# Handing the sums of x and the residual add of an LSTM to GpSimd, step by step

## The chip, the cores and the metric

The kernel runs on one core of one Trainium2 chip. The metric is the device time of one execution in microseconds (us). A core has a matrix engine (TensorE, PE in the profile, its weight loads shown apart as PEld), VectorE (DVE), ScalarE (ACT), GpSimd (POOL) and SyncE (SP), which here issues the transfers of x and of the output. The engines run their own instruction streams and meet at semaphores.

## The reference

An LSTM layer over 512 steps with a residual: `x` is 32 x 512 x 512 (batch, time, features), the state has 512 features, the weights are 512 x 2048 each.

```python
xW = einsum('ntd,dk->tnk', x, Wx) + b
def step(carry, xw_t):
    prev_h, prev_c = carry
    a = xw_t + prev_h @ Wh
    i, f, o = sigmoid(a[:, :H]), sigmoid(a[:, H:2*H]), sigmoid(a[:, 2*H:3*H])
    g = tanh(a[:, 3*H:])
    next_c = f * prev_c + i * g
    next_h = o * tanh(next_c)
    return (next_h, next_c), next_h
out = x + transpose(hs, (1, 0, 2))
```

Step t+1 cannot begin its product with `Wh` before step t has its `h`. The product with `Wx` does not depend on `h` and can be made ahead.

## The kernel before, in words

**Layout.** Batch (32) and the four blocks of 128 features share the 128 partitions, so a step's `h` is a 128x128 tile. Every float32 operand of a product is split in two float16 parts, "hi" and "lo" (the remainder), and hi·hi, hi·lo and lo·hi are added up in PSUM.

**Two products per step.** `recur` (L240) is the product with `Wh`: 96 matmuls of 256 columns, first for the gates i and f (bank `if_even` or `if_odd`), then for o and g (bank `og_even` or `og_odd`). It waits for `hT_hi`, the transposed float16 part of the last `h`, and before its third block of 16 matmuls for `hT_lo`, the transposed remainder. The product with `Wx` (`product`, L207) is made for two steps (a pair) at a time with seven half-size products instead of eight, Strassen-Winograd fashion. It needs, besides the blocks A11, A12, A21, A22 of x, the sums S1 to S4: S1 = A21 + A22, S3 = A11 - A21, S2 = S1 - A11, S4 = A12 - S2. The seven products are 24 matmuls each, 168 for a pair. They are spread after the `recur` of each of the two steps: `middle` and `close_odd` after an even step, `close_even` and `open_pair` after an odd one.

**What makes x ready.** Steps are counted s = 0 to 7 in a chunk of 8; a group is 4 steps, and `x_ring` holds 4 chunks, loaded by SyncE. For the group two ahead, ScalarE copies 128x512 of x to `x_now` (`copy_x`), VectorE transposes its two halves into `x_blocks` (`transpose_x`, L443) at steps 0 and 1 of a group, forms S1 and S3 at step 1 (`combine_first`) and S2 and S4 at step 2 (`combine_rest`), all by line 454. Later ScalarE casts the blocks to `xT_hi` (`cast_early`, `cast_late`), and VectorE takes the remainders `xT_lo` (`rest_early` L465, `rest_late` L471).

**The step on VectorE** (`step`, L492) in program order: f_c = f·c (L497), i_g = i·g (L499), c_state (L501), a PSUM addition for the Winograd sums (L478 or L489), h_hi = o·tanh(c) in float16 (L509), its transpose hT_hi (L440), h_full, the same product in float32 (L512), h_lo = h_full - h_hi (L515), its transpose hT_lo (L440), another PSUM addition (L484, even steps), the remainders of x (L473 or L468), and then the work for x ahead. At the fourth step of a group one instruction of 128x512 adds the four `h_full` tiles onto the ring (L535) and releases the output transfers.

```python
ring = x_ring[:, ring_of(group)]
nc.vector.tensor_tensor(ring, ring, h_full[:, :, :].rearrange("p r f -> p (r f)"),
                        ALU.add).then_inc(out_ready, GROUP)
```

**What sets the order.** All is written out by hand; each engine runs its instructions in the order of the text, and counting semaphores hold the engines together. SyncE waits for `out_ready` to reach a whole chunk before it stores it. GpSimd has no work. Before the steps there is a part in which VectorE and ScalarE split the weights in hi and lo.

Of the kernel before, what the change touches and what calls it, by code (L numbers as in the profile page):

```python
# [10 lines left out]
P = 128  # L11
# [26 lines left out]
def lstm_residual(nc, x, h0, w_x, w_h, bias, out):  # L38
# [20 lines left out]
    with ExitStack() as ctx:  # L59
# [6 lines left out]
        def sem(name):  # L66
            return ctx.enter_context(nc.semaphore(name))
# [49 lines left out]
        c_zeroed = sem("c_zeroed")  # L117
        x_now_ready = sem("x_now_ready")
        x_blocks_ready = sem("x_blocks_ready")
        early_hi_ready = sem("early_hi_ready")  # L120
        early_ready = sem("early_ready")
        late_hi_ready = sem("late_hi_ready")
# [28 lines left out]
        def steps(engine, step, body=CHUNK, begin=0):  # L151

            with nc.Fori(begin, T // body - 1, engines=(engine,), hint_back_edge=True) as c:
                for s in range(body):
                    step(c * body + s, s, body, c)
            for s in range(body):
                step(T - body + s, s, body - 1 - s, T // body - 1)

        def ring_of(group):

            return bass.ds(group % (RING // GROUP) * (GROUP * P), GROUP * P)
# [162 lines left out]
        def _(act):  # L324
# [10 lines left out]
                nc.scalar.activation(x_now[:, :], x_ring[:, ring_of(group)], ACT.Copy).then_inc(x_now_ready, 1)  # L335

            def cast_early(group, pair):
                act.wait_ge(x_blocks_ready, group * 6 + 6)
                nc.scalar.activation(xT_hi[:, pair % 2, EARLY, :], x_blocks[:, pair // 2 % 2, pair % 2, F_EARLY, :],
                                     ACT.Copy).then_inc(early_hi_ready, 1)  # L340

            def cast_late(group, pair):
                act.wait_ge(x_blocks_ready, group * 6 + 6)
                nc.scalar.activation(xT_hi[:, pair % 2, LATE, :], x_blocks[:, pair // 2 % 2, pair % 2, F_LATE, :],  # L344
                                     ACT.Copy).then_inc(late_hi_ready, 1)

            def step(t, s, left, c):
# [20 lines left out]
                if s % GROUP == 0 and left >= CHUNK:  # L368
                    if s == 0:
                        act.wait_ge(x_loaded, (c + 2) * X_DMA)  # L370
                    act.wait_ge(x_blocks_ready, (c * 2 + s // GROUP) * 6 + 12)
                    copy_x(c * 2 + s // GROUP + 2)
                if s % 2 == 0 and left >= 5:
                    act.wait_ge(a22_done, q + 1)
# [62 lines left out]
        def _(dve):  # L437
            def transpose_h(ready, part, to, done, count):
                dve.wait_ge(ready, count)
                nc.vector.transpose(to[:, :].rearrange("p (k e) -> p k e", k=J),  # L440
                                    part[:, :].rearrange("p (e k) -> p k e", k=J)).then_inc(done, 1)
# [6 lines left out]
                dst = x_blocks[:, g % 2, :, first:first + 5:4, :]  # L448
                nc.vector.transpose(dst, src[:, :, odd, :, :]).then_inc(x_blocks_ready, 1)  # L449

            def combine(group, g, to, a, b, op, after):
                blocks = x_blocks[:, g % 2, :, :, :]
                dve.wait_ge(x_blocks_ready, group * 6 + after)
                nc.vector.tensor_tensor(blocks[:, :, to, :], blocks[:, :, a, :], blocks[:, :, b, :],  # L454
                                        op).then_inc(x_blocks_ready, 1)

            def combine_first(group, g):
                combine(group, g, S1, A21, A22, ALU.add, 2)
                combine(group, g, S3, A11, A21, ALU.subtract, 2)

            def combine_rest(group, g):
                combine(group, g, S2, S1, A11, ALU.subtract, 3)
                combine(group, g, S4, A12, S2, ALU.subtract, 5)

            def rest_early(q, pair):  # L465

                dve.wait_ge(early_hi_ready, q + 1)
# [24 lines left out]
            def step(t, s, left, c):  # L492
# [15 lines left out]
                if left:  # L508
                    nc.vector.tensor_tensor(h_hi[:, :], o_gate[:, :], tanh_c[:, :],  # L509
                                            ALU.mult).then_inc(h_hi_ready, 1)  # L510
                    transpose_h(h_hi_ready, h_hi, hT_hi, hT_hi_ready, t + 2)
                nc.vector.tensor_tensor(h_now, o_gate[:, :], tanh_c[:, :], ALU.mult).then_inc(h_full_ready, 1)  # L512
                dve.wait_ge(h_full_ready, now)
                if left:
# [9 lines left out]
                if left >= CHUNK:  # L524
                    ahead, g = group + 2, s // GROUP
                    if s % GROUP == 0:
                        transpose_x(ahead, g, 0)
                    if s % GROUP == 1:
                        transpose_x(ahead, g, 1)
                        combine_first(ahead, g)  # L530
                    if s % GROUP == 2:
                        combine_rest(ahead, g)
                if s % GROUP == GROUP - 1:
                    ring = x_ring[:, ring_of(group)]
                    nc.vector.tensor_tensor(ring, ring, h_full[:, :, :].rearrange("p r f -> p (r f)"),  # L535
                                            ALU.add).then_inc(out_ready, GROUP)

            def split_lo(src, hi, lo):
                return nc.vector.scalar_tensor_tensor(out=lo, in0=src, scalar=WSCALE, in1=hi,  # L539
# [33 lines left out]
            for group in range(2):  # L573
                transpose_x(group, group, 0)
                transpose_x(group, group, 1)
                combine_first(group, group)
                combine_rest(group, group)
            for pair in range(2):
                rest_early(pair, pair)
                rest_late(pair, pair)  # L580
# [38 lines left out]
                split_h_lo(k)  # L619
            rest_early(2, 2)  # L620
            dve.wait_ge(c_zeroed, 1)
            steps(mybir.EngineType.DVE, step)


# [20 lines left out]
```

## Time and profile before

| what | value |
|---|---|
| median of 3 runs | 2577.95 us (2577.83 to 2578.16) |
| the profiled execution's own time | 2577.3 us |
| its span in the trace | 2575.5 us |
| TensorE busy | 2528.3 us (98%) |
| VectorE busy | 1959.4 us (76%) |
| ScalarE busy | 1023.6 us (40%) |
| GpSimd busy | 0.2 us (0%) |
| mean granted TensorE clock | 0.991 of full speed |

The span runs from the first to the last instruction of one profiled execution. The execution's own time is 1.8 us more, and the median of the unprofiled runs 0.65 us above that. Busy shares are means over the whole span. The slice table of the page shows that all slices look alike after the first, which holds the splitting of the weights (PE at 4 tenths there and at 9 after it).

### The profile page before, as it was taken

How to read it: one execution, taken by the hardware profiler on the slowest of the kernel's cores; microseconds unless marked ns; L12 is line 12 of the kernel's file. 1: busy time of each engine (PE TensorE's matmuls, PEld its weight loads, DVE VectorE, ACT ScalarE, POOL GpSimd, SP SyncE). 2: the span in 40 equal slices, each digit the busy share in tenths (PEclk: the TensorE clock that was granted, in tenths of full speed). 3: DMA queues.
4: the chain of work that ended last, by engine and by line, in shares of the span. 5: the costliest groups of instructions: out<-in, count | busy, mean ns of one | idle time of the engine just before them, and what ended most of it. 6: DMA issues, size and time to landing. Idle time of an engine off the chain costs nothing.

```text
span 2575.5 us, 201412 instructions
## 1 busy us (share of the span) xinstructions
PE 2528.3 (98%) x92166; PEld 2445.7 (95%) x92166; DVE 1959.4 (76%) x6328; ACT 1023.6 (40%) x3231; POOL 0.2 (0%) x4
## 2 busy tenths in 40 slices
PE   4999999999999999999999999999999999999998
PEld 3999999999999999999999999999999999999997
DVE  8777777777777777777777777777777777777775
ACT  5334343333433433343334334333433333343342
POOL 0000000000000000000000000000000000000000
PEclk6999999999999999999999999999999999999999
DMA  4011010010110110100101101101101011011000
GB/s 169 18 33 32 16 33 24 24 33 16 33 33 16 33 33 16 33 24 24 33 19 30 33 16 33 33 16 33 27 22 33 22 27 33 16 33 33 16 16 18
DMA packets 141209, 76.17 MB, mean 30 GB/s; under 512 B 8452, under 2 KB 140164, under 8 KB 140164
## 3 DMA queue, kind: packets, MB, share of 16 engines
q1 hardware_dynamic: 140480, 75.53, 11.0%
q10 hardware_dynamic: 708, 0.33, 0.1%
q8 instruction: 17, 0.28, 0.0%
q14 instruction: 4, 0.03, 0.0%
HBM read 42.27 MB, written 33.55 MB: 29 GB/s over the span
## 4 chain that ended last, share of the span: by engine, by line
PE 98%; DVE 2%; issue 0%; DMA 0%; ACT 0%; ACTq 0%; DVEq 0%
PE if_odd L214 26%; PE if_odd L221 13%; PE og_odd L221 13%; PE og_even L221 13%; PE if_even L221 13%; PE s1t_sum L214 7%; PE if_even L214 6%; PE og_even L214 6%; DVE xw_lo L539 1%; DVE w_raw L564 0%; DVE hw_lo L539 0%; DMA h_raw<-in_cond_dram 0%; DVE x_blocks L449 0%; DVE x_blocks L454 0%; ACTq L394 0%
## 5 line engine op out<-in xcount | busy, mean ns | idle before, releaser
L499 DVE TENSOR_TENSOR i_g<-i_f,g_gate 128x128 f32<-128x128 f32 x512 | 149.7, 292 | 429.4 <-ACT g_gate L354 429.4
L214 PE MATMUL if_odd<-xw_hi,xT_hi 128*32 128x256 f16 x8192 | 403.1, 273 | 29.9 <-DVE xw_lo L539 24.3
L214 PE MATMUL if_odd<-xw_lo,xT_hi 128*32 128x256 f16 x8192 | 403.0, 273 | 0.0
L214 PE MATMUL if_odd<-xw_hi,xT_lo 128*32 128x256 f16 x8192 | 403.0, 273 | 0.0
L214 PEld LDWEIGHTS if_odd<-xw_hi,xT_hi 128*32 128x32 f16 x8192 | 219.8, 97 | 36.5 <-DVE xw_lo L539 31.8
L362 ACT ACTIVATE tanh_c<-c_state 128x128 f32<-128x128 f32 x512 | 158.5, 310 | 193.6 <-DVE c_state L501 193.6
L214 PEld LDWEIGHTS if_odd<-xw_lo,xT_hi 128*32 128x32 f16 x8192 | 220.3, 97 | 5.0
L214 PEld LDWEIGHTS if_odd<-xw_hi,xT_lo 128*32 128x32 f16 x8192 | 220.2, 97 | 5.0
L331 ACT ACTIVATE if_even<-if_odd 128x256 f32<-128x256 f32 x256 | 94.2, 368 | 260.1 <-PE if_odd L214 260.1
L351 ACT ACTIVATE i_f<-if_odd 128x256 f32<-128x256 f32 x256 | 98.7, 386 | 225.5 <-PE if_odd L221 225.5
L344 ACT ACTIVATE xT_hi<-x_blocks 128x256 f16<-128x256 f32 x256 | 106.5, 416 | 192.5 <-PE if_odd L214 192.5
L440 DVE STREAM_TRANSPOSE hT_hi<-h_hi 128x128 f16<-128x128 f16 x512 | 161.1, 315 | 17.4
L440 DVE STREAM_TRANSPOSE hT_lo<-h_lo 128x128 f16<-128x128 f16 x512 | 159.8, 312 | 17.4
L497 DVE TENSOR_TENSOR f_c<-i_f,c_state 128x128 f32<-128x128 f32 x512 | 148.5, 290 | 31.6 <-ACT i_f L351 9.9
L351 ACT ACTIVATE i_f<-if_even 128x256 f32<-128x256 f32 x256 | 98.6, 385 | 180.8 <-PE if_even L221 180.8
L449 DVE STREAM_TRANSPOSE x_blocks<-x_now 128x256 f32<-128x256 f32 x256 | 167.1, 653 | 0.0
L354 ACT ACTIVATE g_gate<-og_odd 128x128 f32<-128x128 f32 x256 | 71.3, 279 | 237.1 <-PE og_odd L221 237.1
L354 ACT ACTIVATE g_gate<-og_even 128x128 f32<-128x128 f32 x256 | 71.2, 278 | 237.1 <-PE og_even L221 237.1
L509 DVE TENSOR_TENSOR h_hi<-o_gate,tanh_c 128x128 f16<-128x128 f32 x511 | 149.1, 292 | 19.2 <-ACT tanh_c L362 0.4
L501 DVE TENSOR_TENSOR c_state<-i_g,f_c 128x128 f32<-128x128 f32 x512 | 149.5, 292 | 17.4
L515 DVE TENSOR_TENSOR h_lo<-h_full,h_hi 128x128 f16<-128x128 f32 x511 | 149.3, 292 | 17.6
L221 PE MATMUL if_even<-hw_lo,hT_hi 128*32 128x256 f16 x4096 | 157.0, 273 | 4.9 <-DVE hw_lo L539 4.8
(78 smaller groups left out, 5812.3 us busy)
## 6 DMA issues: line engine op xcount, KB each, us to landing
x_ring<-in_x_dram SPq DMA_DIRECT2D x256, 128.0 KB, 2.8
out_dram<-x_ring SPq DMA_DIRECT2D x252, 128.0 KB, 2.1
w_raw<-in_L_cond_Wx_dram SPq DMA_DIRECT2D x4, 1024.0 KB, 7.7
w_raw<-in_L_cond_Wh_dram SPq DMA_DIRECT2D x4, 1024.0 KB, 15.5
out_dram<-x_ring SPq DMA_DIRECT2D x8, 64.0 KB, 1.8
bias_raw<-in_L_cond_b_dram ACTq DMA_DIRECT2D x4, 64.0 KB, 4.0
h_raw<-in_cond_dram ACTq DMA_DIRECT2D x1, 64.0 KB
```

What stands on the lines that cost most here:

```text
L214: mm = nc.tensor.matmul(bank[j * N:(j + 1) * N, 0:HALF], x_part[:, pair, n, k * N:(k + 1) * N], w_part[:, n, k, j, :], start=start and g = ...
L221: mm = nc.tensor.matmul(bank[j * N:(j + 1) * N, 0:HALF], hT[:, k * N:(k + 1) * N], w[:, k, j, half * HALF:(half + 1) * HALF], start=False, ...
L351: nc.scalar.activation(i_f[:, :], i_f_bank[:, 0:2 * P], ACT.Sigmoid, scale=UNSCALE).then_inc(if_ready, 1)
L354: nc.scalar.activation(g_gate[:, :], og_bank[:, P:2 * P], ACT.Tanh, scale=UNSCALE).then_inc(g_ready, 1)
L362: nc.scalar.activation(tanh_c[:, :], c_state[:, :], ACT.Tanh).then_inc(tanh_c_ready, 1)
L440: nc.vector.transpose(to[:, :].rearrange("p (k e) -> p k e", k=J), part[:, :].rearrange("p (e k) -> p k e", k=J)).then_inc(done, 1)
L449: nc.vector.transpose(dst, src[:, :, odd, :, :]).then_inc(x_blocks_ready, 1)
L497: nc.vector.tensor_tensor(f_c[:, :], i_f[:, P:2 * P], c_state[:, :], ALU.mult)
L499: nc.vector.tensor_tensor(i_g[:, :], i_f[:, 0:P], g_gate[:, :], ALU.mult).then_inc(i_g_ready, 1)
L501: nc.vector.tensor_tensor(c_state[:, :], i_g[:, :], f_c[:, :], ALU.add).then_inc(c_ready, 1)
L509: nc.vector.tensor_tensor(h_hi[:, :], o_gate[:, :], tanh_c[:, :], ALU.mult).then_inc(h_hi_ready, 1)
L515: nc.vector.tensor_tensor(h_lo[:, :], h_now, h_hi[:, :], ALU.subtract).then_inc(h_lo_ready, 1)
```

## The change

The four sums of x go from VectorE to GpSimd with the same shapes and the same order. Their semaphore is a new one, `x_sums_ready`, for which ScalarE's casts wait; `x_blocks_ready` now counts the transposes alone. The residual addition of 128x512 at every fourth step becomes one of 128x128 at every step, on GpSimd, as soon as that step's `h_full` is there. Since GpSimd reads `h_full` later than VectorE goes on, VectorE waits, before it writes an `h_full` tile again, for the addition of four steps ago. The first chunk of VectorE's steps is written out, so that this wait's value is a positive one.

```diff
             def cast_early(group, pair):
-                act.wait_ge(x_blocks_ready, group * 6 + 6)
+                act.wait_ge(x_sums_ready, group * 4 + 4)
...
-                    act.wait_ge(x_blocks_ready, (c * 2 + s // GROUP) * 6 + 12)
+                    act.wait_ge(x_blocks_ready, (c * 2 + s // GROUP) * 2 + 4)
                     copy_x(c * 2 + s // GROUP + 2)
...
+                if not isinstance(t, int) or t >= GROUP:
+                    dve.wait_ge(out_ready, t - (GROUP - 1))
                 nc.vector.tensor_tensor(h_now, o_gate[:, :], tanh_c[:, :], ALU.mult).then_inc(h_full_ready, 1)
...
                         transpose_x(ahead, g, 1)
-                        combine_first(ahead, g)
-                    if s % GROUP == 2:
-                        combine_rest(ahead, g)
-                if s % GROUP == GROUP - 1:
-                    ring = x_ring[:, ring_of(group)]
-                    nc.vector.tensor_tensor(ring, ring, h_full[:, :, :].rearrange("p r f -> p (r f)"),
-                                            ALU.add).then_inc(out_ready, GROUP)
...
+        @block.gpsimd
+        def _(pool):
+            def combine(group, g, to, a, b, op, after):
+                blocks = x_blocks[:, g % 2, :, :, :]
+                if after:
+                    pool.wait_ge(x_sums_ready, group * 4 + after)
+                else:
+                    pool.wait_ge(x_blocks_ready, group * 2 + 2)
+                nc.gpsimd.tensor_tensor(blocks[:, :, to, :], blocks[:, :, a, :], blocks[:, :, b, :],
+                                        op).then_inc(x_sums_ready, 1)
+
+            def combine_first(group, g):
+                combine(group, g, S1, A21, A22, ALU.add, 0)
+                combine(group, g, S3, A11, A21, ALU.subtract, 0)
+
+            def combine_rest(group, g):
+                combine(group, g, S2, S1, A11, ALU.subtract, 1)
+                combine(group, g, S4, A12, S2, ALU.subtract, 3)
+
+            def step(t, s, left, c):
+                now = t + 1 if isinstance(t, int) else pool.snap(t + 1)
+                if left >= CHUNK and s % GROUP == 1:
+                    combine_first(c * 2 + s // GROUP + 2, s // GROUP)
+                if left >= CHUNK and s % GROUP == 2:
+                    combine_rest(c * 2 + s // GROUP + 2, s // GROUP)
+                pool.wait_ge(h_full_ready, now)
+                ring = x_ring[:, bass.ds(c % SLOTS * (CHUNK * P) + s * P, P)]
+                nc.gpsimd.tensor_tensor(ring, ring, h_full[:, s % GROUP, :], ALU.add).then_inc(out_ready, 1)
+
+            for group in range(2):
+                combine_first(group, group)
+                combine_rest(group, group)
+            steps(mybir.EngineType.Pool, step)
```

On VectorE, in the loop over the steps, at step 1 of a group (`i_g`, `f_c`, `h_full` and the like are the tiles named above; "waits" names the semaphores of an instruction). Before:

```order
L440 STREAM_TRANSPOSE hT_hi<-h_hi 128x128 [waits h_hi_ready]
L512 TENSOR_TENSOR h_full<-o_gate,tanh_c 128x128
L515 TENSOR_TENSOR h_lo<-h_full,h_hi 128x128 [waits h_full_ready]
L440 STREAM_TRANSPOSE hT_lo<-h_lo 128x128 [waits h_lo_ready]
L467 REGISTER_ALU
L468 TENSOR_TENSOR xT_lo<-x_blocks,xT_hi 128x192 [waits early_hi_ready]
L449 STREAM_TRANSPOSE x_blocks<-x_now 128x4x64 [waits x_now_ready]
L453 ISA
L454 TENSOR_TENSOR x_blocks<-x_blocks 128x2x64 [waits x_blocks_ready] x2
L497 TENSOR_TENSOR f_c<-i_f,c_state 128x128 [waits if_ready]
```

The same place in the changed kernel (line numbers are the changed kernel's):

```order
L441 STREAM_TRANSPOSE hT_hi<-h_hi 128x128 [waits h_hi_ready]
L500 REGISTER_ALU
L501 TENSOR_TENSOR h_full<-o_gate,tanh_c 128x128 [waits out_ready]
L504 TENSOR_TENSOR h_lo<-h_full,h_hi 128x128 [waits h_full_ready]
L441 STREAM_TRANSPOSE hT_lo<-h_lo 128x128 [waits h_lo_ready]
L454 REGISTER_ALU
L455 TENSOR_TENSOR xT_lo<-x_blocks,xT_hi 128x192 [waits early_hi_ready]
L450 STREAM_TRANSPOSE x_blocks<-x_now 128x4x64 [waits x_now_ready]
L484 TENSOR_TENSOR f_c<-i_f,c_state 128x128 [waits if_ready]
```

Two sums are gone between the transpose of x and f_c, and h_full has a wait and a register instruction that it did not have.

On GpSimd, in its loop, steps 0, 1 and 2 of a group in the changed kernel (L614 is a sum of x, L633 the addition of h onto x; there was nothing here before):

```order
L633 ISA [waits h_full_ready]
L633 TENSOR_TENSOR x_ring<-x_ring,h_full 128x128
L613 ISA
L614 TENSOR_TENSOR x_blocks<-x_blocks 128x2x64 [waits x_blocks_ready] x2
L631 REGISTER_ALU
L633 ISA [waits h_full_ready]
L633 TENSOR_TENSOR x_ring<-x_ring,h_full 128x128
L611 ISA
L614 TENSOR_TENSOR x_blocks<-x_blocks 128x2x64 [waits x_sums_ready]
L611 REGISTER_ALU
L614 TENSOR_TENSOR x_blocks<-x_blocks 128x2x64 [waits x_sums_ready]
```

S1 and S3 stand ahead of step 1's addition of h, and S2 and S4 ahead of step 2's wait for h_full, so that five GpSimd instructions follow one another from the end of the second transpose of x on.

## Rows read from the trace of the kernel before

**Rows 1.** The page: busy times, and the chain that ended last.
```profile
PE 2528.3 (98%) x92166; PEld 2445.7 (95%) x92166; DVE 1959.4 (76%) x6328; ACT 1023.6 (40%) x3231; POOL 0.2 (0%) x4
PE 98%; DVE 2%; issue 0%; DMA 0%; ACT 0%; ACTq 0%; DVEq 0%
```
**Rows 2.** Busy us (and instructions) of each engine in one stretch, then the clock.
```profile
1500.00:2000.00 500.00, 500.00 (x18329) 485.39 (x18324) 381.91 (x1246) 198.54 (x636) 0.00 (x0) 1.00 0.11 27
```
**Rows 3.** Timeline (start us, us, engine, line) where `recur` begins; its blocks.
```profile
1298.85 0.31 DVE L440 STREAM_TRANSPOSE hT_hi<-h_hi 128x128 f16<-128x128 f16 x1
1299.07 0.39 PE L214 MATMUL if_odd<-xw_hi,xT_lo 128*32 128x256 f16 x8
1299.22 0.40 PEld L221 LDWEIGHTS if_even<-hw_hi,hT_hi 128*32 128x32 f16 x16
1299.29 0.61 PE L221 MATMUL if_even<-hw_hi,hT_hi 128*32 128x256 f16 x16
1299.70 0.31 DVE L440 STREAM_TRANSPOSE hT_lo<-h_lo 128x128 f16<-128x128 f16 x1
1300.06 0.43 PEld L221 LDWEIGHTS if_even<-hw_hi,hT_lo 128*32 128x32 f16 x16
1300.16 0.61 PE L221 MATMUL if_even<-hw_hi,hT_lo 128*32 128x256 f16 x16
...
1309.12 0.61 PE L221 MATMUL if_even<-hw_hi,hT_hi 128*32 128x256 f16 x16
```
**Rows 4.** Timeline of the last steps, where TensorE has no other product to make.
```profile
2561.32 0.62 PE L221 MATMUL if_even<-hw_hi,hT_hi 128*32 128x256 f16 x16 [0.40 <-DVE hT_hi L440]
...
2566.17 0.62 PE L221 MATMUL if_odd<-hw_hi,hT_hi 128*32 128x256 f16 x16 [1.39 <-DVE hT_hi L440]
...
2570.72 0.69 DVE L535 TENSOR_TENSOR x_ring<-x_ring,h_full 128x512 f32<-128x512 f32 x1
```
**Rows 5.** VectorE's groups by line and shape: busy us, mean ns.
```profile
L454 DVE TENSOR_TENSOR x_blocks<-x_blocks 128x128 f32<-128x128 f32 x512 | 136.4, 288 | 8.8
L535 DVE TENSOR_TENSOR x_ring<-x_ring,h_full 128x512 f32 x126 | 86.2, 684 | 0.0
```
**Rows 6.** Timeline from step 1's remainder of x to step 2's h_full.
```profile
1300.18 0.36 DVE L468 TENSOR_TENSOR xT_lo<-x_blocks,xT_hi 128x192 f16<-128x192 f32 x1 [0.17 <-ACT xT_hi L339]
1300.46 0.66 DVE L449 STREAM_TRANSPOSE x_blocks<-x_now 128x256 f32<-128x256 f32 x1
...
1300.83 0.39 ACT L351 ACTIVATE i_f<-if_even 128x256 f32<-128x256 f32 x1 [0.68 <-PE if_even L221]
...
1302.45 0.29 DVE L499 TENSOR_TENSOR i_g<-i_f,g_gate 128x128 f32<-128x128 f32 x1 [0.60 <-ACT g_gate L354]
...
1302.77 0.29 DVE L501 TENSOR_TENSOR c_state<-i_g,f_c 128x128 f32<-128x128 f32 x1
...
1302.98 0.42 DVE L478 TENSOR_TENSOR s1t<-s1t_sum,bias_diff 128x256 f32<-128x256 f32 x1
...
1303.10 0.31 ACT L362 ACTIVATE tanh_c<-c_state 128x128 f32<-128x128 f32 x1 [0.52 <-DVE c_state L501]
...
1303.44 0.29 DVE L509 TENSOR_TENSOR h_hi<-o_gate,tanh_c 128x128 f16<-128x128 f32 x1
...
1304.00 0.25 DVE L512 TENSOR_TENSOR h_full<-o_gate,tanh_c 128x128 f32<-128x128 f32 x1
```
**Rows 7.** Timeline of VectorE before the steps, the part with the sums of x.
```profile
10.27 1.14 DVE L449 STREAM_TRANSPOSE x_blocks<-x_now 128x256 f32<-128x256 f32 x2
11.45 1.02 DVE L454 TENSOR_TENSOR x_blocks<-x_blocks 128x128 f32<-128x128 f32 x4
...
13.60 0.42 DVE L582 TENSOR_TENSOR bias_diff<-bias_raw 128x256 f32<-128x256 f32 x1
```
**Rows 8.** Timeline: h_full and h_lo of step 1, ahead of the row of rows 6.
```profile
1299.09 0.25 DVE L512 TENSOR_TENSOR h_full<-o_gate,tanh_c 128x128 f32<-128x128 f32 x1
1299.37 0.29 DVE L515 TENSOR_TENSOR h_lo<-h_full,h_hi 128x128 f16<-128x128 f32 x1
```
**Rows 9.** The only kind of GpSimd instruction in the trace (4 like it).
```profile
0.24 0.10 POOL L635 MEMSET const-float32-0.0<- 128x1 f32 x1 [0.24 <-issue]
```

More of the change, by code:

```diff
@@ L119, in lstm_residual @@
         x_blocks_ready = sem("x_blocks_ready")
+        x_sums_ready = sem("x_sums_ready")
         early_hi_ready = sem("early_hi_ready")
@@ L342, in cast_late @@
             def cast_late(group, pair):
-                act.wait_ge(x_blocks_ready, group * 6 + 6)
+                act.wait_ge(x_sums_ready, group * 4 + 4)
                 nc.scalar.activation(xT_hi[:, pair % 2, LATE, :], x_blocks[:, pair // 2 % 2, pair % 2, F_LATE, :],
@@ L449, in transpose_x @@
                 nc.vector.transpose(dst, src[:, :, odd, :, :]).then_inc(x_blocks_ready, 1)
[L451 to L463, printed above, removed]
             def rest_early(q, pair):
@@ L575, in _ @@
                 transpose_x(group, group, 1)
-                combine_first(group, group)
-                combine_rest(group, group)
             for pair in range(2):
@@ L621, in _ @@
             dve.wait_ge(c_zeroed, 1)
-            steps(mybir.EngineType.DVE, step)
+            for s in range(CHUNK):
+                step(s, s, CHUNK, 0)
+            steps(mybir.EngineType.DVE, step, begin=1)
+        @block.gpsimd
[27 more added lines that the diff above has]
+            steps(mybir.EngineType.Pool, step)
 _INS = ['x', 'cond_1024', 'L0_cond_Wx', 'L0_cond_Wh', 'L0_cond_b']
```

## The prediction

> **What bounds the kernel now.** I read the busy times and the chain of waits first. TensorE is busy 98% of the span, and the chain that ended last runs 98% over TensorE [rows 1]. The table by stretches says that this is no mean over unlike parts: between 1500 and 2000 us TensorE is busy for all of the 500 us, at full clock, while VectorE does 382 us of work [rows 2]. So the steady part goes at the rate of the matmuls: two steps take 9.83 us, from one start of the same block to the next (1299.29 to 1309.12) [rows 3], which is 4.915 us a step.
>
> Next I ask how far the other loop is behind: from `recur` through the gates to the transposed h and back to `recur`. The timeline answers twice. In the steady part hT_hi ends at 1299.16, the weight load that needs it starts 0.06 us later at 1299.22, and its matmuls start at 1299.29, 0.22 us after the product block in front of them, the usual distance between blocks of eight [rows 3]. hT_lo ends at 1300.01, and its weight load comes at 1300.06 and its matmuls at 1300.16 [rows 3]. Both arrive just in time. At the end of the kernel, where TensorE has run out of other products, it waits for hT_hi (1.39 us), and there the starts are 2561.32 and 2566.17 [rows 4]. That is the loop by itself: 4.85 us. **The recurrence has 4.915 - 4.85 = 0.065 us of slack a step.** A busy share of 76% looks like room on VectorE, but what VectorE does between the gates and hT_hi has almost none, and work that is outside of it costs nothing.
>
> **What the change takes away.** VectorE loses 512 sums of 0.288 us, 136.4 us in all, and 128 additions of 0.684 us, 87.5 us (126 of them make 86.2 us) [rows 5]. About 224 us of busy time go. Where did they stand? Between the last transpose of a step and f_c of the next. In the step shown x's transpose ends at 1301.12, i_f of the next step is there at 1301.22, and i_g, the first instruction on the loop, waits for its gate until 1302.45 [rows 6]. The two sums and f_c between them fit into 1.3 us. TensorE waits for none of them. I book their removal in the steady part at 0 us. The cover is the wait for the gate g, and it stays.
>
> Before the steps VectorE is the one that others wait for, so there the sums count. The eight sums take 2 x 1.02 us, and the remainders of x are over at 13.60 [rows 7]. After the change the second pair of transposes no longer waits behind the first four sums, but ScalarE's casts of group 0, and so the remainders, wait for four GpSimd instructions. At the price for one worked out below, these take 1.7 us from about 9.3, so the remainders begin near 11.4 and end near 12.4: a gain of about 1 us. The bounds are a gain of 2.0 us (all eight sums) and a loss of 1 us (remainders held up by GpSimd's second four sums). At the end, the last addition of 0.69 us [rows 4] becomes one of 128x128 on another engine: a gain of 0.2 us at most. Together -1 us.
>
> **What it adds to VectorE's stream.** One register instruction and one wait before h_full. The addition waited for is four steps old, some 19 us, and GpSimd has eight instructions in that time, so the wait is over long before. Does a wait that is already over still cost time on hT_lo's path? The PSUM addition at 1302.98 has a wait that is over and yet starts before c_state in front of it ends at 1303.06, as h_full does now (1299.09, with hT_hi ending at 1299.16) [rows 3, 6, 8]. I book 0. If it did cost the overlap, h_full would start 0.07 us + 0.03 us later, hT_lo has about 0.05 us to give, and 512 steps x 0.05 us would be 26 us. This stays in the range.
>
> **What it adds on GpSimd.** Per group of four steps, four sums and four additions, all of two SBUF operands of 128 columns. The trace has no such instruction on GpSimd. From below the price is VectorE's for the same sum, 0.29 us [rows 5]. From above I take VectorE's for four times the columns, 0.68 us [rows 5]. GpSimd's memset of a single column takes 0.10 us [rows 9], which I take as its fixed part: 0.10 + 0.29 = 0.39, and 0.03 us for the hand-over, **0.42 us** as an estimate, nearest to the lower row because the shape is the same. Eight of them are 3.4 us in 19.7 us. GpSimd is no bound.
>
> The Trainium skill, "GPSIMD Engine Reference", section "Performance versus the Vector engine", gives 4497 ns against 2293 ns for a two-input addition of 2048 columns, 1.96 times VectorE; by that an instruction would take 0.57 us, no run here shows it, and the walk below would come to 1.2 us for a group and 2720 us in all.
>
> **What the two engines do to each other.** This decides, and the trace before cannot show it, since GpSimd never runs beside VectorE. The bounds are nothing (both keep their durations) and full exclusion (of two instructions that both read two SBUF operands, the later waits until the earlier ends). I take exclusion, as both engines then want four operand streams from the same memory at once, and as the loop leaves a slack so small that even a part of it would be seen.
>
> The Trainium skill, "SBUF — State Buffer", section "SBUF: two separate sides", says that VectorE and GpSimd share a port pair, and that a VectorE instruction with two SBUF inputs and a GpSimd one that reads SBUF hold it by turns, each for its whole duration. It speaks against this change, and no run here has shown it yet.
>
> With exclusion, where do they meet? Three steps of four are harmless. The addition of h is released when h_full ends (1299.34), h_lo starts at 1299.37 on the same release [rows 8], and GpSimd, a semaphore away (0.06 us, as for TensorE), comes second. It runs from 1299.66 to 1300.08 under the transpose hT_lo, which has one operand, and is over before the remainder of x at 1300.18 [rows 6]. In step 1, however, the sums go first and wait for the second transpose of x, which ends at 1301.12 [rows 6], and five GpSimd instructions follow each other into step 2's gates. Walked through with 0.42 us:
>
> - S1 from 1301.18 to 1301.60. f_c (ready at 1301.26) waits, 1301.60 to 1301.89. No harm. S3 to 1302.31.
> - The addition of h from 1302.34 to 1302.76. i_g, due at 1302.45 [rows 6], starts at 1302.76: 0.31 late.
> - S2, next in line, from 1303.05 to 1303.47. c_state, due at 1303.08, waits again and starts at 1303.47 instead of 1302.77: 0.70 late.
> - S4 from 1303.76 to 1304.18, mostly under tanh. h_hi is ready at 1304.14 and starts at 1304.18: 0.74 late.
>
> Of 0.74 us the slack takes 0.06. TensorE stops for 0.68 us, and nothing gives it back later, because TensorE is full in the other three steps. There are 126 such groups (the loop's 63 chunks x 2): **126 x 0.68 = 86 us**. The same walk with 0.29 us ends 0.50 late, 55 us; with 0.68 us h_hi is 1.33 late and h_full another 0.4, 210 us.
>
> **Sum.** Against the profiled execution's own time of 2577.3 us: -224 us of busy time worth 0, -1 before and after the steps, +86, 0 for the wait, gives 2662 us. The median of the runs is 0.65 us higher, so 2663 us, 3.3% slower.
>
> **Rivals.**
> - *The engines do not hold each other up*, or it is GpSimd that yields each time. Then TensorE stays full, and only the -1 us is left: 2577 us, within 0.2% (5.2 us, about what a measurement of this kernel can tell from no change). For it: ScalarE works beside VectorE all the time, and VectorE's instructions of one shape keep their 0.29 us [rows 6]. This is the case that ends on the other side: not slower. It decides if the durations of i_g and c_state in step 2, and the gaps before them, are as now. Chance 0.18.
> - *Every step is hit*: GpSimd's addition also keeps the transpose hT_lo waiting. From 1299.66 it would hold it to 1300.08 instead of 1299.70, 0.38 late with 0.05 of slack: 512 x 0.33 = 169 us, with the 86 us of the groups 2830 us, or 2746 us by itself. Against it: the transpose has one operand, and is float16. Chance 0.10.
> - *The new wait costs*: +26 us, 2603 us, where nothing else does. Chance 0.05.
> - *Gain before the steps grows* to over 5.2 us. The eight sums are worth 2.0 us and the tail 0.2, so it would need a faster rate of the steady part, which the matmuls fix. Chance 0.03.
>
> **Chances.** Exclusion at step 2 of each group keeps 0.64; its own range is 2630 to 2740 us, since the walk jumps with the order in which the instructions meet. The range of 8 in 10 reaches down to the case without hold-ups, at 2576 us, and up to 2745 us. It leaves out the top of the walk with 0.68 us and most of the case in which every step is hit. Slower by over 0.2%: 0.64 + 0.10 + 0.05 = 0.79; within 0.2%: 0.18; faster: 0.03.
>
> **What would show it.** In the profile after: TensorE's busy time as before while its idle time before `recur` grows, released by hT_hi, by 0.7 us once in every four steps and nothing in the other three; i_g and c_state of step 2 starting late while their inputs are ready; GpSimd at 1024 instructions. VectorE at about 1735 us confirms only that the work moved. I am wrong if the idle time lies before the weight loads of hT_lo in every step (then it is the addition of h), if a GpSimd instruction takes over 0.6 us, or if TensorE shows no idle time at all.

## The result, and the profile after

| | before | changed |
|---|---|---|
| median of 6 runs | 2577.9 us (2577.22 to 2578.19) | 2588.29 us (2586.78 to 2589.25) |
| ratio | 1 | 1.0041 (95% interval 1.0031 to 1.0052) |
| span of the profiled execution | 2575.5 us | 2586.8 us |

The change costs 10.4 us. The page of the changed kernel, busy times and chain, beside [rows 1]:

```profile
PE 2537.8 (98%) x92166; PEld 2429.7 (94%) x92166; DVE 1818.8 (70%) x5688; ACT 1024.5 (40%) x3231; POOL 475.9 (18%) x1028
PE 97%; DVE 2%; issue 0%; DMA 0%; POOL 0%; ACTq 0%; ACT 0%; POOLq 0%; DVEq 0%
```

VectorE has 640 instructions less and is busy for 140.6 us less. That is not the 224 us that left it: 83 us have come back, and the groups will show where. GpSimd is busy for 476 us. The chain reads almost as before and does not show where the time went. The table by stretches, same stretch and columns as [rows 2], is the view that shows the loss:

```profile
1500.00:2000.00 500.00, 500.00 (x18256) 480.50 (x18248) 353.00 (x1114) 198.05 (x634) 93.77 (x203) 1.00 0.11 27
```

TensorE still counts as busy for the whole 500 us, because a gap of 0.08 us hides under matmuls whose ends overlap (a block of eight is shown as 0.39 us, and the next one starts after 0.22 us). But it finishes 18256 of them instead of 18329, 0.40% less, at the same granted clock (1.00). **Where an engine is the bound, read its instructions per stretch, not its busy share.**

The waits name the place. The line is new in this size (it stood at 1.7 us, once, in the kernel before):

```profile
PEld if_odd L222 <- DVE hT_hi L441: 24.3, 126, 1.7
```

There are 126 waits, of which one, of 1.7 us, was there before. The 125 new ones are one in each group that has sums but for one, all before `if_odd`, that is, between an even and an odd step. VectorE's and GpSimd's groups (busy us, mean ns, idle before):

```profile
L484 DVE TENSOR_TENSOR f_c<-i_f,c_state 128x128 f32<-128x128 f32 x512 | 180.9, 353 | 185.9 <-ACT i_f L352 167.6
L488 DVE TENSOR_TENSOR c_state<-i_g,f_c 128x128 f32<-128x128 f32 x512 | 166.6, 325 | 17.5
L486 DVE TENSOR_TENSOR i_g<-i_f,g_gate 128x128 f32<-128x128 f32 x512 | 150.2, 293 | 434.1 <-ACT g_gate L355 434.1
...
L614 POOL TENSOR_TENSOR x_blocks<-x_blocks 128x128 f32<-128x128 f32 x512 | 250.8, 501 | 787.9 <-DVE x_blocks L450 777.8
L633 POOL TENSOR_TENSOR x_ring<-x_ring,h_full 128x128 f32 x504 | 231.5, 459 | 1280.8 <-DVE h_full L501 1280.8
```

f_c had 290 ns and c_state 292 ns; i_g, h_hi and h_lo are as they were. A mean of 325 ns over 512 instructions hides that only some of them are long, so the view of one tile is worth a look (duration min/median/max):

```profile
L484 DVE TENSOR_TENSOR f_c<-i_f,c_state x512: 291/292/558, 52.5 to 2579.6; 128x128 f32<-128x128 f32 x171
L488 DVE TENSOR_TENSOR c_state<-i_g,f_c x512: 291/292/432, 53.0 to 2581.2; 128x128 f32<-128x128 f32 x171
```

The median is as before: in the trace 125 of the 512 f_c and 126 of the 512 c_state are long, and the others are unchanged. The timeline, from the end of x's second transpose to step 3's `recur`, beside [rows 6]; GpSimd's instructions are shown one by one:

```profile
1307.62 0.65 DVE L450 STREAM_TRANSPOSE x_blocks<-x_now 128x256 f32<-128x256 f32 x1
...
1308.34 0.46 POOL L614 TENSOR_TENSOR x_blocks<-x_blocks 128x128 f32<-128x128 f32 x1 [6.11 <-DVE x_blocks L450]
...
1308.40 0.54 DVE L484 TENSOR_TENSOR f_c<-i_f,c_state 128x128 f32<-128x128 f32 x1
...
1308.76 0.51 POOL L614 TENSOR_TENSOR x_blocks<-x_blocks 128x128 f32<-128x128 f32 x1
...
1309.22 0.46 POOL L633 TENSOR_TENSOR x_ring<-x_ring,h_full 128x128 f32 x1
...
1309.61 0.29 DVE L486 TENSOR_TENSOR i_g<-i_f,g_gate 128x128 f32<-128x128 f32 x1 [0.66 <-ACT g_gate L355]
...
1309.64 0.58 POOL L614 TENSOR_TENSOR x_blocks<-x_blocks 128x128 f32<-128x128 f32 x1
...
1309.93 0.43 DVE L488 TENSOR_TENSOR c_state<-i_g,f_c 128x128 f32<-128x128 f32 x1
...
1310.30 0.46 POOL L614 TENSOR_TENSOR x_blocks<-x_blocks 128x128 f32<-128x128 f32 x1
...
1311.14 0.39 PE L215 MATMUL if_odd<-xw_hi,xT_lo 128*32 128x256 f16 x8
...
1311.44 0.62 PE L222 MATMUL if_odd<-hw_hi,hT_hi 128*32 128x256 f16 x16
```

Reading it as sums of start and duration: S1 ends at 1308.80 and f_c at 1308.94, **0.14 us behind it**. S2 ends at 1310.22 and c_state at 1310.36, again 0.14 us behind. i_g overlaps with the last 0.07 us of the addition (to 1309.68) and is not late at all. S2 itself, which starts 0.03 us behind i_g, takes 0.58 us instead of the 0.46 us of S1, so GpSimd is held up by VectorE as well. `recur` starts 0.30 us after the block in front of it instead of 0.22. So a group loses 0.08 us, and 126 x 0.08 = 10 us is the result.

Before the steps the gain that I had booked is not there. VectorE begins the weights at 14.79 instead of 14.26, 0.53 us late, of which 0.46 us was there at its first instruction already (the transfer of the starting h landed later). The remainders of x, which met GpSimd's second four sums, are long (0.67 us for two of them), which leaves a loss of 0.07 us.

### The profile page after: what moved, and what is told of

It reads as the page before. It is cut to its first block, busy times and chain, and to the rows that moved or that the text cites. A ratio compares the mean times of both kernels' runs of the same rounds, so it can differ in the third digit from the quotient of the medians.

```text
span 2586.8 us, 203038 instructions
## 1 busy us (share of the span) xinstructions
PE 2537.8 (98%) x92166; PEld 2429.7 (94%) x92166; DVE 1818.8 (70%) x5688; ACT 1024.5 (40%) x3231; POOL 475.9 (18%) x1028
## 4 chain that ended last, share of the span: by engine, by line
PE 97%; DVE 2%; issue 0%; DMA 0%; POOL 0%; ACTq 0%; ACT 0%; POOLq 0%; DVEq 0%
PE if_odd L215 26%; PE if_odd L222 13%; PE if_even L222 13%; PE og_even L222 13%; PE og_odd L222 13%; PE s1t_sum L215 6%; PE if_even L215 6%; PE og_even L215 6%; DVE xw_lo L521 1%; DVE hw_lo L521 0%; DVE w_raw L546 0%; DMA h_raw<-in_cond_dram 0%; ACTq L395 0%; POOL x_blocks L614 0%; DVE xT_lo L455 0%
## 5 line engine op out<-in xcount | busy, mean ns | idle before, releaser
L633 POOL TENSOR_TENSOR x_ring<-x_ring,h_full 128x128 f32 (+1 forms) x512 | 235.9, 461 | 1318.6 <-DVE h_full L501 1318.6
L614 POOL TENSOR_TENSOR x_blocks<-x_blocks 128x128 f32<-128x128 f32 x512 | 250.8, 501 | 787.9 <-DVE x_blocks L450 777.8
L484 DVE TENSOR_TENSOR f_c<-i_f,c_state 128x128 f32<-128x128 f32 x512 | 180.9, 353 | 185.9 <-ACT i_f L352 167.6
L488 DVE TENSOR_TENSOR c_state<-i_g,f_c 128x128 f32<-128x128 f32 x512 | 166.6, 325 | 17.5
```

The source lines that it names most:

```text
L484: nc.vector.tensor_tensor(f_c[:, :], i_f[:, P:2 * P], c_state[:, :], ALU.mult)
L488: nc.vector.tensor_tensor(c_state[:, :], i_g[:, :], f_c[:, :], ALU.add).then_inc(c_ready, 1)
L614: nc.gpsimd.tensor_tensor(blocks[:, :, to, :], blocks[:, :, a, :], blocks[:, :, b, :], op).then_inc(x_sums_ready, 1)
L633: nc.gpsimd.tensor_tensor(ring, ring, h_full[:, s % GROUP, :], ALU.add).then_inc(out_ready, 1)
```

## The experiments

### Undoing the change by parts

After the result the theory was: two instructions exclude each other while their operands stream, and only the meeting of S2 with c_state costs. The rivals were the new wait on VectorE and the additions at every step. All four kernels ran on the same chip.

**S2 and S4 behind step 2's addition.** One statement of GpSimd's `step` moves:

```diff
-                if left >= CHUNK and s % GROUP == 2:
-                    combine_rest(c * 2 + s // GROUP + 2, s // GROUP)
                 pool.wait_ge(h_full_ready, now)
...
                 nc.gpsimd.tensor_tensor(ring, ring, h_full[:, s % GROUP, :], ALU.add).then_inc(out_ready, 1)
+                if left >= CHUNK and s % GROUP == 2:
+                    combine_rest(c * 2 + s // GROUP + 2, s // GROUP)
```

> The changed kernel with one thing moved: at step 2 of a group GpSimd first waits for h_full and adds h, and forms S2 and S4 after that. Theory (a GpSimd instruction that reads SBUF and a VectorE one with two SBUF operands exclude each other while their operands stream, and in the change S2 stretches c_state of step 2 from 0.29 to 0.43 us, of which the slack takes 0.06): c_state is back at 0.29 us in every step, TensorE's stop of 0.08 us per group goes, and the time is that of before, 2577 to 2579 us. Rival (the wait for out_ready, or the additions at every step, cost it): the time stays at about 2588 us.

Measured: 2577.34 us, ratio 1.0 (0.9991 to 1.0009). The stretch and the groups:

```profile
1500.00:2000.00 500.00, 500.00 (x18332) 485.17 (x18324) 351.43 (x1118) 198.84 (x636) 93.01 (x204) 1.00 0.11 27
```
```profile
L484 DVE TENSOR_TENSOR f_c<-i_f,c_state 128x128 f32<-128x128 f32 x512 | 182.2, 356 | 187.0 <-ACT i_f L352 170.0
L488 DVE TENSOR_TENSOR c_state<-i_g,f_c 128x128 f32<-128x128 f32 x512 | 149.6, 292 | 17.4
```

c_state is back at 292 ns and TensorE at 18332 matmuls in the stretch, with all of the work still on GpSimd. f_c is stretched as in the change, and that costs nothing. This is what the whole offload is worth when it costs nothing: VectorE 30 us less in 500, and the time of before.

**Only the additions on GpSimd.** The sums are VectorE's again, as in the kernel before, with the semaphores of the casts; GpSimd keeps `step` without them. The edit is shown against the changed kernel, as in the next run:

```diff
                         transpose_x(ahead, g, 1)
+                        combine_first(ahead, g)
+                    if s % GROUP == 2:
+                        combine_rest(ahead, g)
...
-                if left >= CHUNK and s % GROUP == 1:
-                    combine_first(c * 2 + s // GROUP + 2, s // GROUP)
-                if left >= CHUNK and s % GROUP == 2:
-                    combine_rest(c * 2 + s // GROUP + 2, s // GROUP)
                 pool.wait_ge(h_full_ready, now)
```

> Only the additions of h go to GpSimd (with their wait on VectorE); the sums of x stay on VectorE. Theory: each addition runs beside h_lo and comes second, so nothing on VectorE's loop is held up: 2577 to 2579 us. Rival (the wait or the additions cost): 2588 us. A VectorE sum may meet an addition in step 1, without harm.

Measured: 2577.89 us, ratio 1.0 (0.9991 to 1.0009). 512 additions on GpSimd and the wait cost nothing.

**Only the sums on GpSimd.** The addition of 128x512 is VectorE's again, without the new wait, and GpSimd's addition of h is left out:

```diff
-                if not isinstance(t, int) or t >= GROUP:
-                    dve.wait_ge(out_ready, t - (GROUP - 1))
...
+                if s % GROUP == GROUP - 1:
+                    ring = x_ring[:, ring_of(group)]
+                    nc.vector.tensor_tensor(ring, ring, h_full[:, :, :].rearrange("p r f -> p (r f)"),
+                                            ALU.add).then_inc(out_ready, GROUP)
```

> Only the sums of x go to GpSimd; the addition of h stays on VectorE as one of 128x512, and VectorE has no new wait. Theory: the sums alone reproduce a loss, and since S2 and S4 follow S1 and S3 without an addition between them, S4 now meets c_state (due 1.66 us after x's second transpose) a little deeper: c_state of step 2 ends 0.1 to 0.25 us late, 0.04 to 0.19 us past the slack, 126 times: 2583 to 2602 us. Rival (wait or additions cost): 2578 us.

Measured: 2587.69 us, ratio 1.0038 (1.0024 to 1.0052). The sums alone make the whole loss. Now it is S4 that meets c_state, as its timeline shows:

```profile
1310.49 0.46 POOL L614 TENSOR_TENSOR x_blocks<-x_blocks 128x128 f32<-128x128 f32 x1
...
1310.66 0.43 DVE L488 TENSOR_TENSOR c_state<-i_g,f_c 128x128 f32<-128x128 f32 x1
```

S4 ends at 1310.95 and c_state at 1311.09, 0.14 us behind. That the loss is the same as the change's is a coincidence: in both kernels a GpSimd instruction ends 1.95 us after x's transpose, four sums of 0.46 to 0.5 us here, and in the change S1, S3, the addition of h and an S2 that i_g has stretched by 0.12 us.

**Only the wait.** The kernel before, with the wait and with VectorE's first eight steps written out (not shown); GpSimd is idle:

```diff
+                if not isinstance(t, int) or t >= GROUP:
+                    dve.wait_ge(out_ready, t - (GROUP - 1))
                 nc.vector.tensor_tensor(h_now, o_gate[:, :], tanh_c[:, :], ALU.mult).then_inc(h_full_ready, 1)
```

> The kernel before with nothing but the new wait for out_ready ahead of h_full on VectorE (over long before, since VectorE's own addition releases it) and the first chunk of steps written out. GpSimd has no work. Theory: 2577 to 2579 us. Rival (the wait costs the overlap of h_full with the transpose ahead of it): up to 0.05 us a step, 2588 to 2603 us, with h_full starting after hT_hi's end instead of 0.07 us before it.

Measured: 2577.73 us, ratio 1.0001 (0.9992 to 1.001). The wait costs nothing.

### What the meeting of two instructions costs

These kernels are the one before plus one GpSimd instruction in every step, on scratch (the raw weights, which nobody reads any more by then). Each is released by a register wait on the semaphore named:

```diff
+        @block.gpsimd
+        def _(pool):
+            def step(t, s, left, c):
+                now = t + 1 if isinstance(t, int) else pool.snap(t + 1)
+                if not isinstance(t, int) or t:
+                    pool.wait_ge(pool_done, t)
+                pool.wait_ge(if_ready, now)
+                nc.gpsimd.tensor_tensor(w_raw[:, 2, 0:1024], w_raw[:, 0, 0:1024], w_raw[:, 1, 0:1024], ALU.add).then_inc(pool_done, 1)
```

**A long addition across the gates** (above, released by `if_ready`).

> The kernel before, and on GpSimd in every step one addition of 128x1024 on scratch (two SBUF operands, output used by nobody), released when i_f is there, 1.2 us before i_g is due. An estimate of its length, from GpSimd's 0.46 us for 128 columns and VectorE's ratio of 1024 to 128 columns (1.216 to 0.288 us): 1.9 us or more. Theory (full exclusion while operands stream): i_g waits for its end in every step; i_g's row shows some 1 us or more instead of 0.29, and the time is 512 times 0.6 to 1.4 us higher, 2880 to 3300 us. Rival (the two share the memory's rate, and each is only slowed): i_g and c_state are stretched by at most their own 0.13 us of streaming each, up to 512 x 0.2 us, at most 2680 us.

Measured: 3153.91 us, ratio 1.2236 (1.22 to 1.2271).

```profile
1303.29 2.47 POOL L632 TENSOR_TENSOR w_raw<-w_raw 128x1024 f32<-128x1024 f32 x1 [3.75 <-ACT i_f L352]
```
```profile
1304.45 1.46 DVE L500 TENSOR_TENSOR i_g<-i_f,g_gate 128x128 f32<-128x128 f32 x1 [0.91 <-ACT g_gate L355]
```

The addition ends at 1305.76 and i_g at 1305.91. Sharing is out: i_g, with 0.13 us of operands to stream (VectorE's 128x512 less its 128x128, 0.396 us, is 1.03 ns a column [rows 5]), stood still for more than a microsecond. The time agrees with one instruction held in every step: 576 us over 512 steps are 1.13 us a step.

Here i_g is held in 405 steps. In most of the others, step 2 of a group, the addition comes ahead of f_c and holds it:

```profile
1321.35 2.36 POOL L632 TENSOR_TENSOR w_raw<-w_raw 128x1024 f32<-128x1024 f32 x1 [3.55 <-ACT i_f L352]
```
```profile
1321.39 2.47 DVE L498 TENSOR_TENSOR f_c<-i_f,c_state 128x128 f32<-128x128 f32 x1
```

The two views also show the other direction. Where the addition comes first it takes 2.36 us, and where f_c is 0.04 us ahead of it, as in the step at 1303.29, it takes 2.47.

**A long copy** (one operand read), against the long addition:

```diff
-                nc.gpsimd.tensor_tensor(w_raw[:, 2, 0:1024], w_raw[:, 0, 0:1024], w_raw[:, 1, 0:1024], ALU.add).then_inc(pool_done, 1)
+                nc.gpsimd.tensor_tensor(w_raw[:, 3, 0:1], w_raw[:, 0, 0:1], w_raw[:, 1, 0:1], ALU.add)
+                nc.gpsimd.tensor_copy(w_raw[:, 2, 0:1024], w_raw[:, 0, 0:1024]).then_inc(pool_done, 1)
```

> As the run with the long addition, but the GpSimd instruction is a copy of 128x1024 from SBUF to SBUF: one operand read, one written (behind an addition of a single column that carries the waits). Theory (any GpSimd instruction that reads SBUF excludes VectorE's with two operands): i_g waits for its end, a smaller loss only because a copy is shorter; 2700 to 3100 us. Rival (only two-operand GpSimd instructions do it): 2577 to 2580 us.

Measured: 2588.47 us, ratio 1.0044 (1.0025 to 1.0064). Neither the size that I expected (2700 to 3100 us) nor the rival's (2577 to 2580 us) came. The copy takes 1.05 us and not 2.45, and in three steps of four it ends 0.11 us after i_g has started and does not stretch it. The mechanism shows at f_c, whose mean goes from 290 to 495 ns, all of it from step 2, where f_c comes second:

```profile
1308.47 1.11 POOL L633 COPY w_raw<-w_raw 128x1024 f32<-128x1024 f32 x1
```
```profile
1308.60 1.12 DVE L498 TENSOR_TENSOR f_c<-i_f,c_state 128x128 f32<-128x128 f32 x1
1309.64 0.28 DVE L500 TENSOR_TENSOR i_g<-i_f,g_gate 128x128 f32<-128x128 f32 x1
```

The copy ends at 1309.58 and f_c at 1309.72, 0.14 us behind. Behind it i_g starts 0.18 us after its gate instead of the usual 0.03, and that 0.15 us is the loss: TensorE's weight loads wait for hT_hi 126 times for 24.3 us, as in the change, and the time is the change's. A GpSimd instruction that reads a single operand excludes VectorE's as well.

**A long memset** (nothing read), against the long copy:

```diff
-                nc.gpsimd.tensor_copy(w_raw[:, 2, 0:1024], w_raw[:, 0, 0:1024]).then_inc(pool_done, 1)
+                nc.gpsimd.memset(w_raw[:, 2, 0:1024], 0.0).then_inc(pool_done, 1)
```

> As the run with the long copy, but the GpSimd instruction is a memset of 128x1024: it writes SBUF and reads nothing. Theory (the exclusion is about reading): 2577 to 2580 us, i_g at 0.29 us. Rival (GpSimd's writes exclude VectorE too): i_g stretched in every step, over 2650 us.

Measured: 2578.07 us, ratio 0.9998 (0.9987 to 1.001). No f_c is over 0.29 us in this run. In the step shown it lies wholly inside the memset:

```profile
1302.17 0.95 POOL L633 MEMSET w_raw<- 128x1024 f32 x1
```
```profile
1302.31 0.28 DVE L498 TENSOR_TENSOR f_c<-i_f,c_state 128x128 f32<-128x128 f32 x1
```

So a GpSimd instruction that writes SBUF and reads nothing does not hold it.

**An addition of 128x512 behind h_full**, where the change has its 128x128, against the long addition:

```diff
-                pool.wait_ge(if_ready, now)
-                nc.gpsimd.tensor_tensor(w_raw[:, 2, 0:1024], w_raw[:, 0, 0:1024], w_raw[:, 1, 0:1024], ALU.add).then_inc(pool_done, 1)
+                pool.wait_ge(h_full_ready, now)
+                nc.gpsimd.tensor_tensor(w_raw[:, 2, 0:512], w_raw[:, 0, 0:512], w_raw[:, 1, 0:512], ALU.add).then_inc(pool_done, 1)
```

> The kernel before, and on GpSimd in every step one addition of 128x512 on scratch, released when h_full is there: four times as many columns as the additions of the change, in the same place. Theory: it starts behind h_lo, runs some 1.3 to 1.7 us beside the transpose hT_lo (one operand, not held), holds up the remainder of x (two operands) by about 1 us, and is over before i_g is due; 2577 to 2585 us, hT_lo's transpose at 0.31 us, the remainder's row at 1 us or more where it follows. Rival (one-operand VectorE instructions are excluded too): hT_lo late by over 1 us in every step, over 3000 us.

Measured: 2577.19 us, ratio 0.9999 (0.9988 to 1.0011). Its timeline shows in one place which VectorE instructions are held:

```profile
1305.63 1.38 POOL L632 TENSOR_TENSOR w_raw<-w_raw 128x512 f32<-128x512 f32 x1 [3.54 <-DVE h_full L513]
```
```profile
1305.58 0.29 DVE L516 TENSOR_TENSOR h_lo<-h_full,h_hi 128x128 f16<-128x128 f32 x1
1305.91 0.31 DVE L441 STREAM_TRANSPOSE hT_lo<-h_lo 128x128 f16<-128x128 f16 x1
1306.14 0.40 DVE L485 TENSOR_TENSOR og_even<-if_odd,s1t 128x256 f32<-128x256 f32 x1
1306.45 0.84 DVE L474 TENSOR_TENSOR xT_lo<-x_blocks,xT_hi 128x256 f16<-128x256 f32 x1
```

h_lo was first and keeps its 0.29 us. The transpose (one operand) and og_even (one operand in PSUM, one in SBUF) run beside the addition at their usual 0.31 and 0.40 us. The remainder of x, with two SBUF operands, takes 0.84 instead of 0.40. It has 256 columns and ends 0.28 us behind the addition (1307.29 and 1307.01), and the remainders of 192 columns end 0.21 to 0.22 us behind. So the time between the two ends grows with VectorE's own columns, by about 1.05 ns each: it is the time in which VectorE streams its operands (1.03 ns a column, above). With this run the prices of an addition by size are 0.46, 1.38 and 2.45 us for 128, 512 and 1024 columns.

**The rule as a forecast.** From the ends above: a VectorE instruction that comes second ends 0.14 us after GpSimd's, so of its own 0.29 us the first 0.15 run under the other, and it is late by (GpSimd's end) - (its due start) - 0.15 us, if that is positive. This is for VectorE instructions of 128 columns. Two additions released by `c_ready`, in the middle of VectorE's loop, test it with a number said ahead. The first has 128 columns, the second 256:

```diff
-                pool.wait_ge(h_full_ready, now)
-                nc.gpsimd.tensor_tensor(w_raw[:, 2, 0:512], w_raw[:, 0, 0:512], w_raw[:, 1, 0:512], ALU.add).then_inc(pool_done, 1)
+                pool.wait_ge(c_ready, now)
+                nc.gpsimd.tensor_tensor(w_raw[:, 2, 0:128], w_raw[:, 0, 0:128], w_raw[:, 1, 0:128], ALU.add).then_inc(pool_done, 1)
```

> The kernel before, and on GpSimd in every step one addition of 128x128 on scratch, released when c_state is there, in the middle of VectorE's loop. The rule from the runs so far: a VectorE instruction with two SBUF operands that meets a running GpSimd one ends 0.14 us after it, so it is late by (GpSimd's end) - (its own due start) - 0.15 us, if that is above 0. GpSimd runs from 0.08 to 0.54 us after c_state's end, h_hi is due at 0.38: late by 0.01 us. Theory: 2577 to 2580 us, although the addition overlaps h_hi in all 511 steps. Rival (an overlap costs what is left of the GpSimd instruction, as the prediction had it: 0.16 us, of which 0.06 is slack): 511 x 0.10 = 51 us, 2629 us.

Measured: 2577.92 us, ratio 1.0002 (0.9992 to 1.0011).

> The same with 128x256: 0.16 us plus 2.3 ns a column (from 0.46, 1.38 and 2.45 us for 128, 512 and 1024 columns) is 0.75 us, from 0.08 to 0.83 us after c_state's end. The rule gives h_hi late by 0.83 - 0.38 - 0.15 = 0.30 us, less 0.06 us of slack, 511 times: +123 us, 2701 us (2690 to 2715), with h_hi's row at 0.59 us. Rival (the prediction's way of pricing): 0.45 - 0.06 = 0.39 us, 511 times: 2777 us. Rival (sharing): at most 0.13 - 0.06, 511 times: 2614 us.

Measured: 2695.75 us, ratio 1.046 (1.0439 to 1.048), against 2701 from the rule, 2777 from the prediction's way of pricing and 2614 from sharing. The two groups of h_hi, 128 columns first:

```profile
L510 DVE TENSOR_TENSOR h_hi<-o_gate,tanh_c 128x128 f16<-128x128 f32 x511 | 159.2, 311 | 20.0 <-ACT tanh_c L363 0.4
```
```profile
L510 DVE TENSOR_TENSOR h_hi<-o_gate,tanh_c 128x128 f16<-128x128 f32 x511 | 298.4, 584 | 19.1 <-ACT tanh_c L363 0.4
```

The first time is not the 2629 us of an overlap that is paid in full. An overlap in all 511 steps costs 0.02 us of lateness, which the slack takes, and nothing in time. 0.27 us more on GpSimd (460 to 731 ns) makes 0.27 us more of h_hi and 118 us of time. (118 / 511 = 0.23 us a step of the 0.29 us by which h_hi is stretched: 0.06 us is the slack once more.)

**The same rule the other way.** No run was made for this; the traces above show it. A GpSimd addition that starts while VectorE is busy with two SBUF operands is longer by what is left of VectorE's instruction, less 0.14 us: S2 by 0.12 us with 0.26 us of i_g left, S3 by 0.05 us with 0.18 us of f_c left, the long addition by 0.11 us with 0.25 us of f_c left, and the addition of h, with 0.14 us of h_lo left, not at all. The change depends on it: with S2 at 0.46 us it would have ended 0.12 us earlier, and by the rule c_state would have been 0.02 us late, within the slack. That last step is worked out and was not run.

## Why the prediction was right or wrong

The forecast was 2663 us (2576 to 2745) with slower at 0.79. The direction was right and the time lies in the range, but the move was +10.4 us against +85 forecast, eight times too large. That the time lies in the range is luck: the range reached down to 2576 us for the sake of the rival without hold-ups, and the mechanism's own range, 2630 to 2740 us, missed it.

- *TensorE's rate is the bound, the slack of the recurrence is 0.065 us*: right. c_state is 0.14 us late and TensorE stops for 0.08. The 0.06 us of the run with 256 columns agrees.
- *224 us off VectorE are worth 0*: right. With S2 and S4 moved, all of it is gone from VectorE and the time is that of before.
- *The wait costs 0*: right, tried alone.
- *The additions of h run behind h_lo and are harmless in three steps of four*: right, tried alone and with four times the columns.
- *GpSimd's price, 0.42 us*: near. The additions take 0.46 us, and the sums 0.46 to 0.58.
- *Before and after the steps -1 us*: wrong by 1 us. The gain was eaten by GpSimd's second four sums meeting the remainders, which I had named as a bound.
- *Exclusion, and its place in step 2*: right in kind. The runs with the long and the 256-column addition rule sharing out.
- **The step that failed is the price of a meeting in the walk through step 2.** I let the whole instruction wait, start and all: c_state "waits again and starts at 1303.47", and likewise f_c, i_g and h_hi, and GpSimd's S3 behind f_c. The runs show that only the streaming of operands excludes. The first 0.15 us of a VectorE instruction overlap with GpSimd's, and the first 0.14 us of a GpSimd addition with VectorE's, so that S3 is hardly moved by f_c (0.51 us instead of 0.46) and S2 loses 0.12 us where the walk had it wait for all of i_g. The meetings of i_g and c_state were so priced 0.15 us too high each, and GpSimd's queue ran late by the same error: in my walk the addition of h ended 1.64 us after x's transpose, in the trace it ended 1.41 us after. i_g, due at 1.34, then meets only 0.07 us of it, below 0.15, and is free. c_state is late by 1.95 - 1.66 - 0.15 = 0.14 us, h_hi, due at 2.47, meets S4's last 0.02 us and is free. Of 0.31 + 0.39 + 0.04 us, 0 + 0.14 + 0 is left.

So the error was not one of rate. Of i_g's 0.31 us, 0.23 go because the addition of h ends earlier, and the last 0.08 lie below 0.15. Of c_state's 0.39 us, 0.15 go by the price and 0.10 because S2 ends 0.32 us behind i_g instead of 0.42. With h_hi's 0.04 us that makes 0.60 of the 0.74 us, and the slack of 0.06 us takes almost half of what remains. The Trainium skill, "SBUF — State Buffer", section "SBUF: two separate sides", has the exclusive lock "for the whole instruction". By that the walk was right, but the measurement decides, and it says that it is not the whole instruction: 0.14 us between the two ends where the held instruction takes 0.29, and 2696 us with 256 columns where the walk's pricing gives 2777. That GpSimd must read SBUF and VectorE must have two SBUF inputs for it, as the same section of the Trainium skill says, the runs agree with: the memset does not hold f_c, and the transpose and the addition from PSUM are not held.

VectorE's missing 83 us are explained only in part by this: the two stretched groups (f_c 32 us, c_state 17 us) make 49 of them, and the remainders of x 1 us. The rest, 33 us, is no loss of time but how busy time is counted: neighbouring instructions overlap by some 0.08 us in the trace, and the engine's busy time counts an overlap once. The traces bear this out. VectorE's durations add up to 2151.9 us before and 1967.6 us after, 192.5 and 148.8 us more than its busy times, and most of the 44 us between these two lies where a sum or a 128x512 addition stood beside a neighbour. Of these, 11 us lie between two sums, which the 224 us counts once already, and 33 are left.

## What to carry to other kernels

Before work is moved to GpSimd, list VectorE's instructions with two SBUF operands on the critical loop, and place GpSimd's reads of SBUF, with their measured lengths (0.46 us for an addition of 128x128), where they end less than 0.15 us after any of these is due (for 128 columns). Count such a read 0.12 us longer if it starts just behind one of them. Behind h_full even 128x512 was free, and one statement moved took away the whole loss. VectorE's busy share says nothing on what relieving it is worth: here 224 us were worth nothing, as its loop was within 0.065 us of a full TensorE. And a full TensorE that loses 0.4% shows it in its instructions per stretch and in its waits, not in its busy time.

## What the hardware showed that I had not expected

- Exclusion is sharp and its tail constant: the held VectorE instruction of 128 columns ended 0.14 to 0.16 us after GpSimd's for GpSimd instructions of 0.46 to 2.47 us, additions and a copy alike. With 192 and 256 columns it ended 0.21 and 0.28 us after. Both engines have a first 0.14 to 0.15 us that overlaps freely.
- A GpSimd addition costs 0.46 us at 128 columns, 0.73 at 256, 1.38 at 512 and 2.45 at 1024, some 2.2 ns a column (the last two include up to 0.11 us for the VectorE instruction just ahead; 1024 columns took 2.36 us where GpSimd came first). VectorE's took 0.29, 0.68 and 1.22 us at 128, 512 and 1024. The ratio grows from 1.6 to 2.0. A copy of 128x1024 took 1.05 us and a memset 0.95 us, less than half of the addition.
